# Attention on one core: the copies of q and of the turned outputs two slots earlier, the turned values and their normalisation one slot later

## What is computed

```
S = 512, H = 16 heads, K = 8 (d_k)
Q, K, V = einsum(x, w_qkv)                       # b h s k
scores  = Q K^T / sqrt(d_k), causal
probs   = softmax(scores)
attn    = probs V
x       = x + attn_cat @ w_o^T
```

## Time and profile before

| what | value |
|---|---|
| runs shown | 1817.78 us median (1813.11 to 1822.81) |
| profiled execution | 1811.78 us, span 1810.0 us |
| mean granted TensorE clock | 0.974 |
| TensorE busy | 93% |
| VectorE busy | 68% |
| ScalarE busy | 56% |
| GpSimd busy | 48% |
| a steady batch of the attention, 1521.2 to 1561.5 us | TensorE 34.80, VectorE 33.29, ScalarE 28.64, GpSimd 10.94 us busy |

### The profile page before, as it was taken

How to read it: one execution, slowest core, us unless ns; L and a number is a source line. 1 busy time by engine, 2 the same in 40 slices (tenths; PEclk the granted TensorE clock), 3 DMA queues, 4 the chain that set the end, 5 groups by cost and what they waited for, 6 DMA issues and landing times. The chain is left out here.

```text
span 1810.0 us, 45237 instructions
## 1 busy us (share of the span) xinstructions
PE 1689.0 (93%) x15966; PEld 996.0 (55%) x15966; DVE 1234.2 (68%) x2880; ACT 1022.0 (56%) x1956; POOL 876.8 (48%) x722
## 2 busy tenths in 40 slices
PE   6899999999998999979999999999898888888888
PEld 4566666666665666646666666666544333333334
DVE  5866666566667888756665666566687877888556
ACT  5655555555555556445555555566433766776633
POOL 2665665675540544566655765674542222222232
PEclk9999999999999999989999999999998999999789
DMA  4200000000000000000000000000001111111000
GB/s 143 91 13 1 0 0 0 0 0 1 1 1 2 2 0 0 2 2 2 1 1 0 0 0 0 0 2 2 1 1 28 45 26 26 25 25 25 1 13 35
DMA packets 14618, 23.41 MB, mean 13 GB/s; under 512 B 2570, under 2 KB 10890, under 8 KB 14356
## 3 DMA queue, kind: packets, MB, share of 16 engines
q1 hardware_dynamic: 14484, 21.62, 4.2%
HBM read 11.00 MB, written 2.10 MB: 7 GB/s over the span
## 5 line engine op out<-in xcount | busy, mean ns | idle before, releaser
L509 POOL TENSOR_TENSOR scratch<-scratch 128x512 f16<-128x512 f32 x384 | 445.4, 1160 | 417.0 <-ACT scratch L670 416.7
L670 ACT ACTIVATE scratch<-scratch 128x512 f16<-128x512 f32 x512 | 322.4, 630 | 441.1 <-DVE scratch L1113 441.0
L1113 DVE SCALAR_TENSOR_TENSOR scratch<-psum,scratch 128x512 f32<-128x512 f32 x512 | 352.8, 689 | 314.0 <-ACT scratch L665 171.6
L1640 PE MATMUL psum<-ffn_down_hi,scratch 128*128 128x128 f16 x2048 | 369.6, 219 | 2.5 <-POOL scratch L509 2.1
L1642 PE MATMUL psum<-ffn_down_hi,scratch 128*128 128x128 f16 x2048 | 369.5, 219 | 0.0
L1641 PE MATMUL psum<-ffn_down_lo,scratch 128*128 128x128 f16 x2048 | 369.3, 219 | 0.0
L665 ACT ACTIVATE scratch<-psum 128x512 f32<-128x512 f32 x512 | 296.4, 579 | 0.2
L1640 PEld LDWEIGHTS psum<-ffn_down_hi,scratch 128*128 128x128 f16 x2048 | 200.1, 98 | 60.4 <-POOL scratch L509 3.1
L1641 PEld LDWEIGHTS psum<-ffn_down_lo,scratch 128*128 128x128 f16 x2048 | 200.2, 98 | 56.3 <-issue 0.3
L1602 PE MATMUL psum<-x_hi,ffn_up_hi 128*128 (+1 forms) x512 | 195.9, 383 | 6.6 <-DVE scratch L1113 6.3
L1642 PEld LDWEIGHTS psum<-ffn_down_hi,scratch 128*128 128x128 f16 x2048 | 200.1, 98 | 0.0
(11 more groups left out here) (231 smaller groups left out, 2954.0 us busy)
## 6 DMA issues: line engine op xcount, KB each, us to landing
raw<-in_ffn_w_dram SPq DMA_DIRECT2D x8, 768.0 KB, 4.3
scratch<-scratch SPq DMA_DIRECT2D x32, 128.0 KB, 2.7
ffn_up_hi<-scratch SPq DMA_DIRECT2D x32, 128.0 KB, 2.7
x_tok<-in_x_dram SPq DMA_DIRECT2D x8, 256.0 KB, 6.4
out_dram<-x_tok SPq DMA_DIRECT2D x8, 256.0 KB, 2.0
raw<-in_lin_dram SPq DMA_DIRECT2D x1, 1092.0 KB
half_sb<-in_half_dram SPq DMA_DIRECT2D x1, 544.0 KB, 5.8
con_sb<-in_con_dram SPq DMA_DIRECT2D x1, 410.5 KB, 5.1
```

What stands on the lines that cost most here:

```text
L509: pool.tensor_tensor(h_lo[r], h32[r], h_hi[r], ALU.subtract).then_inc(s_plo, 1)
L670: act.activation(h_hi[k % HSLOTS], h32[k % HSLOTS], ACT.Copy).then_inc(s_hhi, 1)
L1113: dve.scalar_tensor_tensor(h32[k % HSLOTS], bank(5 + k % 2), W_DOWN, gate_act[k % 2], ALU.mult, ALU.mult).then_inc(s_h, 1)
L1640: pe.matmul(dst, h_hi[r][:, cols], hi, start=k % FC == 0 and n == 0, stop=False, skip_group_check=True)
```

## The change

Seven conditions in the hand-written orders change; no instruction is added or taken away. On ScalarE `q_high` and `out_high` go from behind exponential 8 to behind exponential 6 (so ahead of `values`), and `v_copy` from behind exponential 10 to behind exponential 9. On VectorE `q_low` and `out_low` go from behind maximum 4 to behind maximum 3, and `normalise` from behind maximum 4 to behind maximum 5 and its combine. On TensorE `v_proj` goes from slot 9 to slot 8 and `transpose_values` from slot 8 to slot 9, ahead of `prep_transpose` in g3.

```diff
@@ ScalarE
-                            if t == 8 and g == 0 and more:
+                            if t == 6 and g == 0 and more:
                                 q_high(b + 1)
...
-                            if t == 10 and g == 1 and more:
+                            if t == 9 and g == 1 and more:
                                 v_copy(b + 1, 1 - odd)
-                            if t == 8 and g == 2 and not first:
+                            if t == 6 and g == 2 and not first:
                                 out_high(b - 1)
@@ VectorE
-                            if n == 4 and g == 0 and more:
+                            if n == 3 and g == 0 and more:
                                 q_low(b + 1)
-                            if n == 4 and g == 2 and not first:
+                            if n == 3 and g == 2 and not first:
                                 out_low(b - 1)
...
-                            if n == 4 and not (first and g == 0):
+                            if n == 5 and not (first and g == 0):
                                 normalise(u - 1, b - (g == 0), (g - 1) % NG, odd ^ (g == 0))
@@ TensorE
-                            if t == 9 and g == 1 and more:
+                            if t == 8 and g == 1 and more:
                                 pe.wait_ge(s_mTc, u + 2)
                                 v_proj(b + 1)
...
+                            if t == 9 and follows:
+                                transpose_values(u - 1)
                             if t == 9 and g == 3 and prep:
...
                                 prep_transpose(n0 + SUB * b + LEAD, 7)
-                            if t == 8 and follows:
-                                transpose_values(u - 1)
```

## The result

The changed kernel takes 1824.24 us (median, 1818.61 to 1827.16) against 1817.22 us of the kernel before (1806.89 to 1824.05): ratio 1.0036, 95% interval 1.0021 to 1.0050. The same kernel measured again, beside others, gave 1.0042 (1.0020 to 1.0065), as expected (1.002 to 1.005). It is slower by 0.36%, some 6.5 us. The forecast was 1825, +8 us.

The account below looks back on a forecast made before the run. The prediction took each unit to be bound by a loop of normalisation, PV0 (first weighted-values product), by_query(1) and maxima; its terms summed to +8.1 us, scaled to 1825 us, with own range 1818 to 1832 and wide range 1807 to 1836.

Parts of the forecast that it names:

- 18.1 us of waits: TensorE's waits for out_low (7.5 us), q_low (7.4) and the turned values' copy (3.2), the most that could come back.
- The signs that the prediction named: Near-zero waits before L1602; 0.3 to 1 us for L1513 in most units; period up 0.5 to 0.9; L1503 0.17.
- g0, loop: First four-head unit of batches 1 to 6: first weighted-values product 0.1 us earlier each, -0.6 us in all.
- k_high: ScalarE's k copy about 0.6 us earlier, sparing the second unit's slot 2 0.35 us (bounds 0 and 0.56).
- g3: Fourth four-head unit of a batch: later normalisation delays the first weighted-values product 0.5 us, +3.0 over six batches.
- The delay: From the end of a VectorE instruction to the TensorE instruction waiting for it, taken as 0.06 us.
- The masks beside the combine: GpSimd masks hold L1503, now ahead of the normalisation: +1.8 us each in the first batch's and last batch's affected unit.
- The tail: Last batch's third and fourth units, without maxima: turned values in slot 9 give -0.6 us, bounds 0 and -1.4.
- meet the masks in the steady g2: Slower rival: in every batch's third unit a GpSimd mask holds the combine up to 1.1 us; 1832 us, chance 0.25.
- The faster case: Rival: VectorE finishes units earlier, removed waits come back in good part; about -12 us, 1806, chance 0.15.
- Nothing moves: Rival: TensorE's work between first weighted-values products covers the normalisation, gains and losses cancel; about 1818 us, chance 0.20.
- The clock: Filled TensorE waits should give back half-clock stretches, of the order of 1 us; the forecast gave nothing back.

## Why the prediction was right, point by point

**The bound.** That PV0 would wait for the normalisation is shown twice: by the brackets of the trace and by the two kernels that move it alone, in either direction (+15 us into the kernel before, -20 us and more out of the changed one). The fear that the 18.1 us of waits wouldn't come back was right only because of it: without the late normalisation the copies gave 10 us. The signs that the prediction named are there: no wait before L1602, 26 waits before PV0 of up to 1.1 us between 1376 and 1700 us, the combine of g2 at 0.17 us, and the period up by 0.6 us in the loop; in the written-out batches it is up by 0.3 only, under the 0.5 to 0.9.

**The terms.** Read from PV0 to PV0, at full clock but for the last row:

| term | predicted us | measured us |
|---|---|---|
| g0, loop | -0.1 | +0.03 |
| g1, with k_high | +0.5 - 0.35 = +0.15 | +0.03 |
| g2 | +0.15 | +0.23 |
| g3 | +0.5 | +0.3 (9.86 against 9.54) |
| first batch, g1 | +0.5 | +0.41 (10.79 against 10.38) |
| first batch, g2 | +1.8 | +0.97 (9.85 against 8.88) |
| last batch, g0 | +0.4 | +0.39 (8.89 against 8.50) |
| last batch, g1 | +1.8 | +1.24 (10.55 against 9.31) |
| last batch, tail | -0.6 | +0.15 for g2 (12.64 against 12.49) |

*k_high* was worth 0.54 by the trace, near its upper bound of 0.56: maximum 1 of g1 came 3.00 us after PV0 before (1527.12 to 1530.12) and comes 2.46 after it now; with g1 at +0.03 that leaves 0.57 for its normalisation. This split is a reading of two traces, not shown by a run: moved alone, the normalisation made g1 0.32 us longer (10.89) and the copies made it 0.23 shorter (10.34). *The delay* from VectorE's end to PV0 was taken as 0.06 us from out_low. In the written-out batches it is that (0.05 to 0.06; 1712.78 + 0.29 = 1713.07 to 1713.13 above), but in the hardware loop it is 0.13 to 0.14 behind L1513. That is the missing 0.1 in g0 and g2, and with 0.08 in each of four units it is also the difference between +0.6 us a batch in the loop and +0.3 in batches 5 and 6. Why the loop takes longer there is not shown. *g3* was too dear by 0.2. *The masks beside the combine*: the mechanism held and the size didn't. I let the combine wait for the whole run of masks. It waits for the one that is running (0.33 and 0.60 us long instead of 0.55 and 0.63 before); in both rows the combine began beside the last mask of the run, so they could not tell the two apart. *The tail* gained nothing in g2; its last unit took 13.45 us against 17.11, but there a stretch of the changed kernel ran at full clock and none of the kernel before, so the term can't be read from it.

The sum of the terms as measured is about +6 against the forecast's +8.1, with errors of both signs; the largest is g3 over its six units, 1.2 us too much. At equal clock the whole kernel is +5 us. The measured +6.5 has some 1.5 us of clock in it (3.5 in the second measurement), to which the prediction gave nothing. So the mechanism is right, and that the number is as near as 1.5 us is in part luck: terms that together are 2 to 3 us too dear stand against the clock that was left out.

**The rivals.** The combine did not meet the masks in the steady g2: it is ahead by 0.06 us, in the trace above; the prediction had it by about 0.02 and called it open. The faster case (VectorE earlier than thought) fell with VectorE's idle time before L1493, which rose from 34.7 to 43.8 us. "Nothing moves" fell with the interval, 1.0021 to 1.0050, and with the kernel that moves the normalisation alone.

**The clock** was given nothing, and there the prediction says too little. Windows of the changed kernel behind batch 0's g2, where PV0 had stood 1.08 us (columns as in the earlier trace rows):

```profile
1420.00:1424.00 4.00, 2.31 (x27) 0.84 (x26) 3.18 (x7) 1.60 (x4) 1.22 (x2) 1.00 0.02 4
1424.00:1428.00 4.00, 4.00 (x25) 0.84 (x20) 1.24 (x2) 1.82 (x4) 0.64 (x1) 0.50 0.00 0
...
1432.00:1436.00 4.00, 3.47 (x18) 1.83 (x16) 1.69 (x2) 1.43 (x5) 0.35 (x1) 0.50 0.00 1
...
1444.00:1448.00 4.00, 3.37 (x29) 1.35 (x26) 3.50 (x5) 3.30 (x7) 0.63 (x1) 1.00 0.11 18
```

The clock fell by 1424 and was back only after 1440; the unit took 14.37 us where it took 9.54. In the second profile of the same kernel the unit took 15.51. Over 1400 to 1700 us the mean granted clock is 0.94, before 0.97, so about 36 us against 18 us of half clock. This explains why two profiled executions can lie 13 us apart while the medians lie 7. But the same unit is slow with the normalisation early as well (14.70 and 15.02 us) and PV0 didn't wait there, so the late normalisation isn't the only cause of that stretch. In one profile each it took 15.13 us in the kernel with the normalisation alone, 9.58 with the copies alone and 9.30 with the turned values alone. What brings it on stays open.

How much of the 6.5 us is clock can be told better from all the executions than from profiles. In its first measurement the changed kernel has 114 us at half clock on the mean, where the kernel before has 110 over all of its executions with a clock on record; in the second it has 116 against 105 beside it. That is 4 and 11 us more, at 0.32 us each 1.3 and 3.5 us. The prediction put what the filled waits give back at the order of 1 us and then at nothing. Where PV0 doesn't take their place they give back more: 9 us of half clock, worth 3 us, with the copies alone, and 14 to 17 us, worth 5, with all of the change but the late normalisation.

## What to carry to other kernels

A wait that ends on the path is worth its time only as far as the next wait allows: before moving a step up, look at the next thing that joins the engines (here PV0) and at the slack that its other inputs have; the normalisation ended 0.4 to 1.1 us before PV0 in the steady units of the kernel before, and 0.9 us of VectorE work put ahead of it ate more than the change won. Undo the parts of a bundle one by one: the copies, the turned values and v were good or harmless, and the normalisation cost more than they gave. And where the granted clock differs from execution to execution, compare kernels at equal clock too, or a change of order gets the clock's part put down to it. Moving a long product past short ones on a full engine (PV0 to slot 3) must be costed by what comes to lie behind the pair.

## What the runs showed of the hardware that was not expected

In the changed kernel TensorE's granted clock was 1.00 from 1420 to 1424 us, in which TensorE was busy 2.31 us of 4, with two idle times of 0.61 and 1.08 us. It was 0.50, the 1.2 GHz level, from 1424 to 1440 us, in which TensorE was busy 3.47 us or more of every 4 by the profile. One us more at half clock cost 0.32 us of this kernel's time.

The combine, a VectorE instruction with two SBUF inputs, ended 0.01 to 0.04 us behind the GpSimd mask beside which it began, in all six places read (the masks of a row taken as equal parts); in the last batch of the changed kernel it ended with the second of three masks and didn't wait for the third. The Trainium skill, "SBUF — State Buffer", section "Who interferes with whom", calls the shared port pair an exclusive lock; the end times here agree.

From the end of L1513 to the start of the PV0 that waits for it took 0.05 to 0.06 us in written-out batches and 0.13 to 0.14 us in batches of the hardware loop.
